# Pair levels in 32x32 tiles, chunk values as paired 64-row products, and a new order of rows and work

## The reference

```
xn = layernorm(x)
x  = x + scan_layer(xn) + top1_experts(xn)          # layer 0
xn = layernorm(x)
x  = x + level_attention(xn) + recurrence(xn)       # layer 1

level_attention:  16 heads, state 64, value width 8
  Q, K, V, dl, dt from x;  g = A * softplus(dt);  cg = cumsum(g)
  Lam = softplus(Lp * dl)                            # 12 levels per head and token
  W[t,s] = (Q_t . K_s) / 8 * exp(cg_t - cg_s) * Lam[t, level(t, s)]      (s <= t)
  level(t, s) = 0 if s == t else floor(log2(s xor t)) + 1
  out = layernorm(W V Wout + x) * g + b
```

## Time and profile before

| what | value |
|---|---|
| median of 3 runs | 1076.66 us (1075.57 to 1076.85) |
| profiled execution, its own time | 1077.35 us |
| its span (first to last instruction) | 1075.7 us |
| PE busy | 1028.9 us (96%) |
| DVE busy | 890.4 us (83%) |
| ACT busy | 693.4 us (64%) |
| POOL busy | 247.9 us (23%) |
| mean granted TensorE clock | 0.995 |

### The profile page before, as it was taken

How to read it: one execution, slowest core, us unless ns; L and a number is a source line. 1 busy time by engine, 2 the same in 40 slices (tenths; PEclk the granted TensorE clock), 3 DMA queues, 4 the chain that set the end, 5 groups by cost and what they waited for, 6 DMA issues and landing times. The chain is left out here.

```text
span 1075.7 us, 18976 instructions
## 1 busy us (share of the span) xinstructions
PE 1028.9 (96%) x6188; PEld 667.0 (62%) x6188; DVE 890.4 (83%) x2038; ACT 693.4 (64%) x1509; POOL 247.9 (23%) x235
## 2 busy tenths in 40 slices
PE   7999999999999999999999999999999999999985
PEld 3666657566665766657566665766657566565763
DVE  5897897979889797987979889797987979889776
ACT  4693857749386592957749385683947649385682
POOL 0040310313122031311303131031311203131186
PEclk9999999999999999999999999999999999999998
DMA  4000000000000000000000000000000000000535
GB/s 150 21 1 10 2 20 11 0 29 0 19 10 19 10 0 29 0 19 10 0 29 0 26 4 19 10 0 29 0 19 10 10 20 0 29 0 19 175 108 157
DMA packets 31907, 27.61 MB, mean 26 GB/s; under 512 B 1552, under 2 KB 25744, under 8 KB 31760
## 3 DMA queue, kind: packets, MB, share of 16 engines
q1 hardware_dynamic: 31888, 27.37, 7.9%
HBM read 15.57 MB, written 11.80 MB: 25 GB/s over the span
## 5 line engine op out<-in xcount | busy, mean ns | idle before, releaser
L1765 POOL TENSOR_TENSOR pair<-pair,cgt 128x512 f32<-128x512 f32 x64 | 88.9, 1417 | 505.1 <-DVE pair L1527 505.1
L992 ACT ACTIVATE gx<-p 128x512 f32<-128x512 f32 x256 | 145.8, 596 | 25.8 <-PE p L546 21.3
L544 PE MATMUL p<-x1Th,Gl 128*128 128x512 f32 x256 | 119.9, 468 | 0.3 <-ACT gx L992 0.3
L947 ACT ACTIVATE gelu<-p,bias_u 128x512 f32<-128x512 f32 x32 | 22.0, 687 | 141.9 <-PE p L491 141.9
L546 PE MATMUL p<-x1Th,Gh 128*128 128x512 f32 x256 | 100.8, 394 | 0.0
L545 PE MATMUL p<-x1Tl,Gh 128*128 128x512 f32 x256 | 100.2, 392 | 0.0
L655 PEld LDWEIGHTS p<-vbd,pair 128*128 128x128 f32 x512 | 62.0, 191 | 40.4 <-issue 26.8
L1795 POOL TENSOR_TENSOR skip<-skip,W 128x512 f32<-128x512 f32 x15 | 19.2, 1281 | 275.1 <-DVE skip L1310 275.1
L604 PE MATMUL p<-rs,GT 128*128 128x120 f32 x512 | 65.3, 281 | 15.9 <-ACT rs L1063 11.9
L604 PEld LDWEIGHTS p<-rs,GT 128*128 128x128 f32 x512 | 59.6, 191 | 31.8 <-ACT rs L1063 24.8
L655 PE MATMUL p<-vbd,pair 128*128 128x128 f32 x512 | 73.3, 286 | 0.0
(11 more groups left out here) (270 smaller groups left out, 2657.9 us busy)
## 6 DMA issues: line engine op xcount, KB each, us to landing
xin<-in_x SPq DMA_DIRECT2D x16, 256.0 KB, 2.7
hx_scratch<-vdw SPq DMA_DIRECT2D x15, 256.0 KB, 2.6
res_scratch<-res SPq DMA_DIRECT2D x14, 256.0 KB, 2.1
gx<-in_weights SPq DMA_DIRECT2D x1, 1216.0 KB, 9.9
vp<-hx_scratch SPq DMA_DIRECT2D x4, 256.0 KB, 3.5
GT<-res_scratch SPq DMA_DIRECT2D x4, 256.0 KB, 3.1
out<-vp SPq DMA_DIRECT2D x4, 256.0 KB, 3.4
W<-in_weights SPq DMA_DIRECT2D x1, 746.0 KB, 11.1
```

Of the source, the lines that this page charges most:

```text
L544: pe.matmul(head_bank(h)[:, :], tile(Gl, h), x1Th[:, :], start=True, stop=False)
L992: act.activation(tile(gx, h, T), head_bank(h)[:, :], ACT.Copy).then_inc(R["gx_copied"], 1)
L1765: pool.tensor_tensor(pw, pw, spread(cgt[:, H * n:H * n + H].unsqueeze(2), [128, H, CHUNK]), ALU.subtract)\
```

## The change

`pair_levels` is no longer one product per tile of tokens with a stationary of 128x128, but two calls (half 0 and 1), each of eight products of 32 rows and 32 columns: two row groups (tile 2 * half and the one after it, into banks P1[2] and P1[0]) times four column groups. Half 0 stands where pair_levels(0) stood, half 1 between the second and the third group of node_matrices, whose banks are now 4, 3, 4, 3. For this the tokens of a tile of layer 1's level columns are taken in another order: ScalarE writes a second copy of the turned x1, `x1P`, in which a row block holds one chunk of each of the four tiles, and `values` makes its last 96 columns (the levels 0 to 5) from x1P and the first 336 from x1T. The columns of Wvdw are put in a new order at the start (four copies on VectorE).

`pair_weights` is split: `pair_lams` multiplies by the levels and `pair_weights` by the scores. `chunk_values` is eight products instead of four, each of 64 rows and 64 moving columns, two row halves side by side into the banks P1[3] and P1[2]; `own_heads` reads both, in two instructions. In the loop body VectorE does stats2 and level_weights later, scans is split in two, and ScalarE does two of the four pair_distance before the copies of the last two heads, takes rs copies and decays in turns, and does rstd2 after them. `last()` gets a similar order.

```diff
 def values(j):                                              # PE
-                for n, free in enumerate(("dlam_ready", "ym_ready", "yt_ready", "x1Th_ready")):
+                for n, free in enumerate(("ym_ready", "ym_ready", "yt_ready", "x1Th_ready")):
...
-                    pe.matmul(P1[(2 + n) % 5][:, 0:VDW], tile(x1T, n), w("Wvdw"), start=True, stop=True)\
+                    bank = P1[(2 + n) % 5]
+                    pe.matmul(bank[:, 0:336], tile(x1T, n), w("Wvdw", 0, 336), start=True, stop=True)
+                    if n == 0:
+                        pe.wait_ge(R["x1P_ready"], j + 1)
+                    pe.matmul(bank[:, 336:VDW], tile(x1P, n), w("Wvdw", 336, VDW), start=True, stop=True)\
                         .then_inc(R["vdw_ps"], 1)
 def node_matrices(i):                                       # PE
                 for g in range(4):
-                    if g == 3:
-                        pe.wait_ge(R["m_copied"], 4 * i + 1)
-                    bank = P1[(4, 0, 3, 4)[g]]
+                    if g == 2:
+                        pair_levels(i, 1)
+                    if g >= 2:
+                        pe.wait_ge(R["m_copied"], 4 * i + g - 1)
+                    bank = P1[(4, 3)[g % 2]]
-            def pair_levels(i, n):
-
-                if n == 0:
+            def pair_levels(i, half):
+
+                pe.wait_ge(R["ident_loaded"], 16)
+                if half == 0:
                     pe.wait_ge(R["lev_abs"], i + 1)
+                    pe.wait_ge(R["r_copied"], 4 * i + 2)
                     pe.wait_ge(R["nodesT_ready"], i + 1)
                 else:
-                    pe.wait_ge(R["dlam_ready"], 4 * i + n)
-                pe.matmul(P1[2][:, :], k("left"), tile(nodesT, n, 512), start=True, stop=True).then_inc(R["lam_ps"], 1)
+                    pe.wait_ge(R["dlam_ready"], 4 * i + 2)
+                for c in range(4):
+                    for n in (2 * half, 2 * half + 1):
+                        rows, cols = slice(32 * n, 32 * n + 32), slice(32 * c, 32 * c + 32)
+                        mm = pe.matmul(P1[(2, 0)[n % 2]][cols, :], k("left")[rows, rows], tile(nodesT, c, 512)[rows, :],
+                                       start=True, stop=True)
+                mm.then_inc(R["lam_ps"], 1)
 def levels(i, n):                                           # PE
+                else:
+                    pe.wait_ge(R["dlam_ready"], 4 * i + 4)
 def chunk_values(i, n):                                     # PE
+                else:
+                    pe.wait_ge(R["dlam_ready"], 4 * i + 3)
...
-                    mm = pe.matmul(tile(P1[3], g), pair[:, at:at + 128], vbd[:, at:at + 128], start=True, stop=True)
+                    for half in range(2):
+                        rows, cols = slice(64 * half, 64 * half + 64), slice(at + 64 * half, at + 64 * half + 64)
+                        mm = pe.matmul(tile(P1[3 - half], g, 64), pair[rows, at:at + 128], vbd[rows, cols], start=True, stop=True)
 def chunk_order(i):                                         # ACT, new, between turned1 and high_part
+                act.activation(view(x1P[:, :], "p (c k t) -> p c k t", c=4, k=TILES),
+                               view(P1[0][:, :], "p (k c t) -> p k c t", k=TILES, c=4), ACT.Copy).then_inc(R["x1P_ready"], 1)
 def stages(i, j):                                           # ACT
+                    pair_distance(i, 0, 2)
                     heads(i, 14, H)
+                    pair_distance(i, 2, TILES)
+                    pair_decay(i, 0, 2)
+                    left_halves(i, 0, 3)
+                    pair_decay(i, 2, 3)
+                    left_halves(i, 3, TILES)
+                    pair_decay(i, 3, TILES)
                     if later(i):
                         rstd2(i - 1)
-                    pair_distance(i)
-                    left_halves(i, 0, 2)
-                    pair_decay(i)
-                    left_halves(i, 2, TILES)
                     own_values(i)
                     node_matrices(i)
 def pair_lams(i, n) / pair_weights(i, n)                    # DVE
+            def pair_lams(i, n):
+                dve.wait_ge(R["decay_ready"], 4 * i + n + 1)
+                dve.wait_ge(R["lam_ps"], 2 * i + n // 2 + 1)
+                dve.tensor_tensor(tile(pair, n, 512), tile(pair, n, 512), P1[(2, 0)[n % 2]][:, :], ALU.mult)\
+                    .then_inc(R["dlam_ready"], 1)
 def own_heads(i, n):                                        # DVE
+                for half in range(2):
+                    at = 512 * (n % 2) + 256 * half
+                    last = dve.tensor_tensor(view(ym[:, at:at + 256], "p (m a e) -> p m a e", m=8, a=4),
+                                             view(P1[3 - half][:, 0:256], "p (m a e) -> p m a e", m=8, a=4),
+                                             spread(k("own_head").unsqueeze(1).unsqueeze(3), [128, 8, 4, HD]), ALU.mult)
 def stages(i, j):                                           # DVE
                 if j is not None:
                     delta(j)
                 if i is not None:
-                    level_weights(i)
+                    node_lams(i)
+                    node_rows(i)
+                if j is not None:
+                    scan_inputs(j)
+                    scans(j)
+                if i is not None:
+                    pair_lams(i, 0)
+                    pair_weights(i, 0)
+                    pair_lams(i, 1)
                     if later(i):
                         stats2(i - 1)
...
+                    pair_lams(i, 2)
+                    pair_lams(i, 3)
+                if j is not None:
+                    scan_outs(j)
                     top1(j)
+                if i is not None:
+                    level_weights(i)
                 if i is not None:
                     own_heads(i, 0)
                     pair_weights(i, 1)
 def last():                                                 # DVE
-                level_weights(i)
                 dve.wait_ge(R["c_ready"], B)
                 node_lams(i)
+                node_rows(i)
                 cell_out()
-                node_rows(i)
+                pair_lams(i, 0)
                 pair_weights(i, 0)
+                for n in range(1, TILES):
+                    pair_lams(i, n)
+                level_weights(i)
```

More of the change, by code:

```diff
@@ L154, in build @@
         x1T = sb("x1T", T)
+        x1P = sb("x1P", T)
         VDW = 432
@@ L887, in first @@
                 turned1(0)
+                chunk_order(0)
                 high_part(0)
@@ L965, in turned1, with chunk_order @@
                 act.activation(x1T[:, :], P1[0][:, :], ACT.Copy).then_inc(R["x1T_ready"], 1)
+            def chunk_order(i):
+                if later(i):
+                    act.wait_ge(R["vdw_ps"], 4 * i)
+                act.wait_ge(R["x1T_ps"], i + 1)
+                act.activation(view(x1P[:, :], "p (c k t) -> p c k t", c=4, k=TILES),
+                               view(P1[0][:, :], "p (k c t) -> p c k t", k=TILES, c=4), ACT.Copy).then_inc(R["x1P_ready"], 1)
             def high_part(i):
@@ L1150, in stages @@
                     turned1(j)
+                    chunk_order(j)
                     high_part(j)
@@ L1174, in last @@
                 heads(i, 11, H)
-                pair_distance(i)
-                left_halves(i, 0, 2)
-                pair_decay(i)
-                left_halves(i, 2, TILES)
+                pair_distance(i, 0, TILES)
+                pair_decay(i, 0, 2)
+                left_halves(i, 0, 3)
+                pair_decay(i, 2, 3)
+                left_halves(i, 3, TILES)
+                pair_decay(i, 3, TILES)
                 own_values(i)
@@ L1515, in level_weights @@
                 for n, at in enumerate((0, 128)):
[L1516 to L1520 removed]
+                    dve.scalar_tensor_tensor(rows(tile(alpha, n, 64), 1)[:, 0], rows(e4[:, at:at + 64], 1)[:, 0],
+                                             k("alpha_mask", TILES * n, TILES * n + 1), high[:, n], ALU.mult, ALU.mult)
+                for n in (2, 3):
+                    last = dve.tensor_tensor(rows(tile(alpha, n, 64), 1)[:, 0], rows(e4[:, 64 * n + 64:64 * n + 128], 1)[:, 0],
+                                             high[:, n], ALU.mult)
+                last.then_inc(R["alpha_steps"], 1)
             def token_rows(i):
@@ L1528, in token_rows @@
                     .then_inc(R["cgrow_ready"], 1)
+            def pair_lams(i, n):
[3 more added lines that the diff above has]
+                    .then_inc(R["dlam_ready"], 1)
             def pair_weights(i, n):
-                dve.wait_ge(R["decay_ready"], 4 * i + n + 1)
-                dve.wait_ge(R["lam_ps"], 4 * i + n + 1)
-                dve.tensor_tensor(tile(pair, n, 512), tile(pair, n, 512), P1[2][:, :], ALU.mult)\
-                    .then_inc(R["dlam_ready"], 1)
                 dve.wait_ge(R["s_ps"], 4 * i + n + 1)
@@ L1634, in stages @@
                 if i is not None:
-                    level_weights(i)
```

(20 more changed lines are left out.)

80 lines of the change are left out of this document (41 added, 39 removed).

## The result

| what | before | after |
|---|---|---|
| median of 4 runs each, side by side | 1076.7 us (1075.57 to 1076.85) | 1137.4 us (1137.16 to 1137.88) |
| ratio, 95% interval | | 1.0567, 1.0548 to 1.0585 |
| span of the profiled execution | 1075.7 us | 1135.6 us |
| PE busy | 1028.9 us | 1044.5 us |
| one stage of the loop body | 64.26 us | 68.27 us |

The change makes the kernel 5.7% slower. I had forecast slower, 1104.7 us, with a range to 1124: the direction and the place were right, and half of the size was missing. The same stage as in the rows of before begins at 522.08 in the new trace, 23.80 us later, so that 546.02 here is 522.22 on the prediction's clock.

A forecast was written before the change was run, and what follows sets the result against it. TensorE sets the pace, leaning next on ScalarE's queue. Fourteen stages at +1.95 us (27.3), first stage -0.4, start +1.2 and last stage 0 give +28.1, hence 1104.7 us; range 1093 to 1124.

The forecast's parts named there:

- The chain: Loop body: late statistics make ScalarE wait in rstd2, delaying own_values and ms copies; TensorE gap 3.95 us, stage +1.95 us.
- rival 4: In pair_levels the tiles run row group by row group: +6 us; part of the forecast's chance, 0.59.
- from the start of chunk_values(0) to out0: TensorE's stretch behind the gap: 17.27 us before, 14.92 us forecast, with three pair_levels gone and 0.5 us of waits added.
- the 0.52 us behind out0: Loop stage's end: shape changes around the last chunk_values add 0.30 us, the split of values 0.22 us.
- The failed step: TensorE behind the gap: third and fourth node_matrices groups take 0.89 + 1.08 us, pair_scores(1) ends at 534.05.
- rival 1: TensorE's clock falls in gap, costing 1 to 2 us a stage; 1119 to 1133 us in all stages; chance 0.27.
- The first stage: Stage i = 0, which has no rstd2(i - 1), comes out some 0.4 us shorter.
- the start: Before the loop, four small VectorE copies with waits, about 0.3 us each, add 1.2 us.
- the last stage: VectorE saves some 2 us but GpSimd's sums and the stores come later: taken as 0, bounds -2.5 and +1.2.
- Nothing for chunk_values: TensorE's halved products in chunk_values gain nothing: 0.11 us each, still 1.0 us.
- Rival 2: Row tiling gives chunk_values the promised half price: 25 us less, 1080 us; chance 0.05.
- Rival 3: Statistics are ready when ScalarE asks, so no gap opens: -5.6 us, 1072 to 1074 us; chance 0.09.

The follow-up runs named there:

- gap_filled: Changed kernel with four extra unused 512-column products filling TensorE's gap in each loop stage, ScalarE's wait left in; 1107.25 us.
- before_rstd_late: Kernel before the change, with only stats2 moved behind scans and rstd2 moved to just ahead of own_values; 1179.75 us.
- stats_early: Changed kernel with VectorE doing stats2 ahead of node_lams, ScalarE's order left as changed; 1070.56 us.
- rstd_last: Changed kernel with ScalarE doing rstd2 behind node_matrices instead of ahead of own_values; 1067.7 us.
- gap_half_filled: Changed kernel with two extra unused 512-column products in TensorE's gap in each loop stage; 1122.86 us.
- last_reordered: Changed kernel with rstd2 behind node_matrices, whole chunk_values products, stats2 ahead of node_lams, and last()'s level_weights and cell_out as before the change; 1065.64 us.
- best_order: Changed kernel with rstd2 behind node_matrices, whole chunk_values products, and last()'s level_weights and cell_out as before the change; stats2 stays as changed; 1062.82 us.
- rstd_last_full_products: Changed kernel with rstd2 behind node_matrices, and chunk_values, own_heads and chunk_sums as before the change; 1063.97 us.

## Why the prediction was right and where it was wrong

**The chain held, step by step.** On the prediction's clock (23.80 less): the first half of pair_levels at 522.2 (I had 522.4); node_rows starts at 518.6, so that node_lams is done at 518.55 (518.2), having paid for level_values as bounded; stats2 at 526.2 (525.95); ScalarE idles 3.84 us (about 3.4); the gap is 3.78 us (3.95), and the third group starts at 531.3 (531.1). One half of pair_levels takes 1.02 us for its sixteen instructions and not 1.7: two row groups stream side by side, so rival 4 is out. Behind the gap the working holds too: from the start of chunk_values(0) to out0 it is 14.95 us (14.92). Only the 0.52 us behind out0 came to 0.26; values cost its 0.23 (0.22), and the other 0.30, for the shapes around the last chunk_values, had been 0.40 by the prediction's own 2 x 0.20.

**The failed step** is how long TensorE's work behind the gap takes: "Third and fourth group end at 533.05 (0.89 + 1.08), pair_scores(1) at 534.05". It took both times at full clock. The two groups took 3.70 us (555.10 to 558.80) instead of 1.97, and pair_scores 1.33 instead of 1.0, since the granted clock was 0.50 until 559.5. So out0 starts at 551.28, where the sum had 547.54 + 1.43 = 548.97; of these 2.3 us the clock makes 2.06 and the later start of the third group 0.2. I had this as rival 1, with a price of 1 to 2 us a fall, chance 0.27, and all stages at 1119 to 1133; I held against it that only sparse work followed the gap in the tail. The trace of after shows that argument to be empty: the granted clock is 0.50 from 552.7 on, while TensorE still idles, 2.4 us before the dense work comes. And gap_filled gives the size: with the gap filled a body stage takes the predicted 66.2 us, without it 68.27. Of the missing 31.8 us (59.9 measured, 28.1 summed) the clock in the body is 27.7.

**The smaller terms.** The first stage came out 1.8 us shorter and not 0.4; the start cost 2.3 and not 1.2; the last stage cost 3.8 and not 0.

At the start the clock shows more than the copies. Ahead of the first heads stands a product that waits for xn (L515, L517 after). It starts at 43.69 where it started at 44.84 (and at 42.82 in before_rstd_late, so this point differs by 2 us between traces of one setup), but TensorE has idled 2.16 us for it instead of 0.81, and from it to the first heads it takes 7.43 us instead of 3.98. The windows behind it, first of before and then of after (columns as in the earlier trace rows):

```profile
44.10:48.80 4.70, 3.28 (x12) 1.85 (x13) 3.91 (x9) 2.88 (x6) 0.00 (x0) 1.00 0.01 3
```

```profile
44.10:51.00 6.90, 6.21 (x17) 4.16 (x16) 3.57 (x11) 3.17 (x6) 0.00 (x0) 0.51 0.01 2
```

All ten traces with the changed setup have this, with a wait of 1.4 to 2.2 us; the two with the setup of before have 0.81 us and a clock that stays up. Why the wait got longer wasn't tried.

For the last stage I had set a save of VectorE against late sums of GpSimd, and had not seen that level_weights would stand beside them. The same last() takes 67.4 us in after, gap_filled and stats_early, where the granted clock stays at 0.50 once it has fallen (from 1105.7 on in after), and 65.4 in rstd_last and gap_half_filled, where it comes back to 1.00 for a while; with the order of last_reordered and best_order it takes 63.7 to 63.8. So about 2.0 of the 3.8 us go with the clock and 1.7 with the order, a second fall of the clock behind TensorE's wait of 2.13 us among them.

**Nothing for chunk_values** was right. One tile's eight pairs take 1.04 us (560.13 to 561.17) and not 0.6; the eight products of before took 1.00. By the Trainium skill, page TensorEngine Tiling (Array Packing), Theoretical Speedup, a contraction of 64 could be up to twice as fast; the measurement decides here. It agrees with the Trainium skill's page TensorE: Matmul & The Clock Gate, LDWEIGHTS, by which the load is paid by columns, and the 128 columns stayed; that it is the load which sets the 1.04 us was not tried by itself. The run with whole products puts the net at a loss of 0.20 us a stage, with VectorE's second instruction in it. Rival 2 is out.

**Rival 3**, statistics ready when ScalarE asks, was rightly held unlikely and nearly rightly priced: stats_early makes that state on purpose and takes 1070.6 us (I had 1072 to 1074).

**Where the change's gain went.** It has one. With rstd2 out of the way, the same kernel is 0.8% faster than before, and with whole products 1.2%. With norm2 moved it is 2.3%, but that last step is not the change's: gate0's second instruction takes 1.57 us beside GpSimd in the kernel before too (at 536.60), and no run moves norm2 there. By the timelines the change's own gain is the shorter pair_levels and the end of TensorE's wait for rs; no run takes the two apart. It was hidden under a wait of ScalarE that none of the new products has anything to do with.

## What to carry to other kernels

When a producer is moved later in one engine's queue, look for its reader in every other queue and ask what stands behind that reader; here a 0.2 us instruction that was not urgent held two urgent ones for 3.8 us. Count a gap on TensorE of this length (3.8 us here) twice, once for itself and once for the work behind it at 1.2 GHz, and if it recurs each stage assume that the clock falls each time; an order that merely shortens the gap may not save the second part. Put small VectorE instructions on SBUF operands where GpSimd is idle, and remember that the instruction which releases GpSimd decides when that is.

## What the runs showed of the hardware that was not expected

- The clock falls and rises once a stage. In after it is at 1.2 GHz in all fourteen body stages, for 6.8 us in twelve and for 3.4 us in two; a stage costs 1.98 to 2.08 or some 1.56 us more than the same one in gap_filled, near to half of what TensorE was busy at the low level (4.40 us in the stage read above, 3.40 in the two). The Trainium skill, page TensorE: Matmul & The Clock Gate, section on oscillation, describes a kernel whose waits bring the clock down in each iteration; the traces here agree, and the filled gap turns it off.
- In gap_half_filled a remaining gap of 1.9 us brought the clock down in ten of fourteen stages and left it up in four, with the same work around it.
- Eight 32x32 tiles of 512 float32 columns, sixteen instructions, take 1.02 us from start to next start (546.02 to 547.04); one whole product, two instructions, took 0.86.
- Two VectorE instructions of 64 columns on SBUF operands take 0.47 us by themselves (555.82) and 2.50 beside GpSimd's (1028.28 above), one of GpSimd's instructions each. One of 512 columns (gate0's second) goes from 0.74 to 1.57 us. pair_lams, which reads PSUM, is not slowed: two take 1.29 us beside GpSimd in last(), at 1027.08 in rstd_last_full_products, and 1.28 in the body without it, at 551.49 in after.
